# Order inside a slot of a 30-step layer-norm/FFN pipeline: TensorE turns before it multiplies, ScalarE scales and copies before SiLU and tanh

## The reference

```
def step(h, _):
    h = h + 0.01 * jnp.tanh(h)
    h = h * jax.nn.sigmoid(h)
    h = _layernorm(h, ln_w, ln_b)
    h = jnp.einsum('bsc,dc->bsd', h, W) + b
    return (h, None)
x, _ = jax.lax.scan(step, x, None, length=N_ITERS)   # N_ITERS = 30
```

## Time and profile before

| | |
|---|---|
| median of three executions | 1294.8 us |
| the profiled execution | 1294.57 us, its span 1292.8 us |
| PE busy | 1257.6 us (97% of the span) |
| DVE busy | 1189.0 us (92%) |
| ACT busy | 1005.8 us (78%) |
| POOL busy | 960.8 us (74%) |
| mean granted PE clock | 0.992 of full speed |

### The profile page before, as it was taken

How to read it: one execution, slowest core, us unless ns; L and a number is a source line. 1 busy time by engine, 2 the same in 40 slices (tenths; PEclk the granted TensorE clock), 3 DMA queues, 4 the chain that set the end, 5 groups by cost and what they waited for, 6 DMA issues and landing times.

```text
span 1292.8 us, 29543 instructions
## 1 busy us (share of the span) xinstructions
PE 1257.6 (97%) x9309; PEld 1122.5 (87%) x9309; DVE 1189.0 (92%) x2808; ACT 1005.8 (78%) x1410; POOL 960.8 (74%) x783
## 2 busy tenths in 40 slices
PE   8899999999999999689999999999999999999998
PEld 7677777777777777489999999999999999999998
DVE  7888888888888877799999999999999999999997
ACT  2455555555555555789999999999999999999995
POOL 3455555544555554489999999999999999999996
PEclk9999999999999999889999999999999999999999
DMA  6111111111111000000000000000000000000004
GB/s 192 42 42 42 49 52 54 48 41 41 41 41 41 0 1 1 1 2 0 0 0 0 0 0 0 0 0 0 0 0 0 0 0 0 0 0 0 0 0 130
DMA packets 29808, 27.71 MB, mean 21 GB/s; under 512 B 3285, under 2 KB 21464, under 8 KB 29656
## 3 DMA queue, kind: packets, MB, share of 16 engines
q1 hardware_dynamic: 29784, 27.41, 6.5%
HBM read 23.21 MB, written 4.19 MB: 21 GB/s over the span
## 4 chain that ended last, share of the span: by engine, by line
PE 83%; DVE 10%; ACT 3%; issue 3%; POOL 0%; DMA 0%; SPq 0%; DVEq 0%; ACTq 0%; POOLq 0%
PE psum L860 33%; PE psum L876 16%; PE psum L856 7%; PE psum L631 4%; PE psum L633 4%; PE psum L632 4%; PE psum L802 4%; PE psum L653 3%; PE psum L648 3%; DVE emb_n L1409 2%; DVE xh_mem L1233 1%; PE psum L642 1%; ACT emb_f L993 1%; PE psum L662 1%; DVE upd L1370 1%
## 5 line engine op out<-in xcount | busy, mean ns | idle before, releaser
L482 POOL TENSOR_TENSOR f_rs<-f_var,half_neg 128x8 f32<-128x8 f32 x240 | 395.1, 1646 | 24.5 <-DVE f_var L1299 5.4
L930 ACT ACTIVATE g_ring<-u_ring 128x1024 f32<-128x1024 f32 x240 | 407.1, 1696 | 3.1 <-DVE u_ring L1274 3.0
L953 ACT ACTIVATE y_all<-psum 128x1024 f32<-128x1024 f32 x240 | 397.2, 1655 | 8.7 <-PE psum L876 8.7
L860 PEld LDWEIGHTS psum<-w_t,y_all 128*128 128x128 f32 x2880 | 382.8, 193 | 9.4
L940 ACT ACTIVATE t_ring<-psum 128x1024 f32<-128x1024 f32 x232 | 388.1, 1673 | 3.0 <-PE psum L860 3.0
L860 PE MATMUL psum<-w_t,y_all 128*128 128x128 f32 x2880 | 388.6, 275 | 0.0
L1262 DVE BATCH_NORM_STATS2 f_stat<-g_ring 128x6 f32<-128x256 f32 x960 | 341.9, 418 | 3.5 <-ACT g_ring L930 3.5
L488 POOL TENSOR_TENSOR h_ring<-g_ring,f_rs 128x640 f32<-128x640 f32 x240 | 302.1, 1259 | 18.8
L1274 DVE SCALAR_TENSOR_TENSOR u_ring<-t_ring,psum 128x1024 f32<-128x1024 f32 x232 | 279.0, 1203 | 0.7 <-ACT t_ring L940 0.7
L876 PE MATMUL psum<-ident,h_ring 128*128 128x128 f32 (+1 forms) x1920 | 252.2, 275 | 2.4 <-issue 2.4
L947 ACT ACTIVATE h_ring<-g_ring,f_rs 128x128 f32<-128x128 f32 x240 | 248.3, 1035 | 1.6 <-POOL f_rs L482 1.6
(11 more groups left out here) (194 smaller groups left out, 2136.0 us busy)
## 6 DMA issues: line engine op xcount, KB each, us to landing
work<-in_adj_dram SPq DMA_DIRECT2D x16, 1024.0 KB, 5.4
x_tok<-in_x_dram SPq DMA_DIRECT2D x16, 256.0 KB, 5.6
out_dram<-y_all SPq DMA_DIRECT2D x7, 512.0 KB, 3.2
work<-in_L_gnn_conv_w_dram SPq DMA_DIRECT2D x1, 1088.0 KB
out_dram<-y_all SPq DMA_DIRECT2D x2, 256.0 KB, 3.5
work<-in_L_gnn_w_ih_dram SPq DMA_DIRECT2D x1, 384.0 KB
work<-in_L_gnn_w_hh_dram SPq DMA_DIRECT2D x1, 192.0 KB
work<-in_L_gnn_W_dram SPq DMA_DIRECT2D x1, 64.0 KB, 5.1
```

The source lines that it names most:

```text
L482: pool.tensor_tensor(f_rs[:, j % 4, :], f_var[:, j % 2, :], half_neg[:, 0:GT], ALU.pow).then_inc(f_pow, 1)
L860: m = pe.matmul(y_ps[k % 2][:, h, C * t:C * t + C], y_all[:, GT * k + NT * h + t, :], w1_t[:] if t < biased else w1c_t[:], start=False, st ...
L930: act.activation(g_ring[j], u_ring[j % 2], ACT.Silu).then_inc(f_silu, 1)
L953: act.activation(y_all[:, GT * j:GT * j + GT, :].rearrange("p t c -> p (t c)"), g_ps[j % 2].rearrange("p h n -> p (h n)"), ACT.Copy).then_ ...
```

## The change

In PE's slot the turns are now written ahead of the products: T(s-6), then P(s). In ACT's slot scale(s-5) and state(s-6) are written first, then silu(s-2), and tanh(s) last. DVE, POOL and the DMA queue are unchanged, and so are all waits and lags. T is line 853 now, P is lines 870 and 874.

```
@@ PE @@
             def slot(it, k):
+                before = earlier(it, k, LAG_T)
+                if before is not None:
+                    i, j, s = before
+                    pe.wait_ge(f_norm, s + 1)
+                    if ACT_TILES[j]:
+                        pe.wait_ge(f_norm_act, act_norms(i, j + 1))
+                    pe.wait_ge(f_norm_dve, dve_norms(i, j) + 1)
+                    wait(pe, f_state, s - 1)
+                    for t in range(GT):
...
+                    m.then_inc(f_turn, 1)
                 if not (isinstance(it, int) and it == 0):
...
                     m.then_inc(f_mm, 1)
-                before = earlier(it, k, LAG_T)
-                if before is not None:
...
-                    m.then_inc(f_turn, 1)
@@ ACT @@
             def slot(it, k):
-                before = earlier(it, k, LAG_S)
-                if before is not None:
-                    silu(*before[1:])
-                if not (isinstance(it, int) and it == ITERS):
-                    tanh(it, k)
                 before = earlier(it, k, LAG_A)
                 if before is not None:
                     scale(*before[1:])
                 before = earlier(it, k, LAG_T)
                 if before is not None:
                     state(*before[1:])
+                before = earlier(it, k, LAG_S)
+                if before is not None:
+                    silu(*before[1:])
+                if not (isinstance(it, int) and it == ITERS):
+                    tanh(it, k)
```

More of the change, by code:

```diff
@@ L841, in slot @@
             def slot(it, k):
+                before = earlier(it, k, LAG_T)
[7 more added lines that the diff above has]
+                    for t in range(GT):
+                        rows = P if t < GT - DVE_TILES[j] else P - 1
+                        m = pe.transpose(g_ps[j % 2][0:rows, t // NT, P * (t % NT):P * (t % NT) + P],
+                                         tiles(h_ring[j % 4])[:, t, 0:rows], ident[:])
+                    m.then_inc(f_turn, 1)
                 if not (isinstance(it, int) and it == 0):
```

## The result

The changed kernel takes 1380.52 us (median of 4, 1379.0 to 1381.57), the kernel before 1294.55 in the same comparison: ratio 1.0661, 95% interval 1.0649 to 1.0674, 86 us slower. Forecast were 1378 and a range of 1360 to 1398.

A forecast was written before the change was run, and what follows sets the result against it. DVE alone was taken to bound the kernel at 3.06 us per slot; after the change a two-slot loop through POOL and ACT needs 3.41. 1294.6 + 81.2 (232 slots) + 2.5 (edges) = 1378 us, range 1360 to 1398.

The forecast's parts named there:

- The bound before: Iterated layer of the kernel before: DVE alone bounds at 3.06 us per slot, ACT 0.01 to 0.02 behind, PE 0.07.
- The loop through POOL and ACT: Sum, variance, power, scale, state, silu, stats, sum two slots on: 6.82 us, 3.41 per slot against 3.06; +81.2 us.
- power to scale: Term of the loop: from the start of POOL's power to the start of ACT's waiting scale, 1.67 us.
- silu to stats: Term of the loop: from the start of ACT's silu to DVE's waiting stats, 1.08 to 1.25 us.
- Silu's delay: On ACT: silu's true time is its record of 1.05 us, not the mid-run record of 1.89.
- long-silu rival: ACT's silu really takes 1.89 us: loop 7.57, 3.79 per slot, +169, 1464 us; chance 0.05.
- The edges: First products behind low-clock turns, and PE entering the last iteration later: +2.5 us for both, bounds -1 and +4.
- The other loops: After the change, loops through PE (3.12 per slot) and through tanh on ACT (3.2) stay hidden behind the first.
- Through PE: ... 6.24, or 3.12 per slot: Sum, DVE's scale, turns, products, tanh, sum two slots on: hidden by ACT's loop; without that cover 14 us.
- The clock rival: PE, idle some 0.4 us per slot, drops to 1.2 GHz: 1930 us throughout, about 1650 for half the time; chance 0.04.
- Not slower: Turns fill PE's 19.2 us wait for the sum: 1278 us, or 1295 if nothing changes; chance 0.06, half each.
- The signs in the profile: Profile after: sums 3.41 apart; ACT idle before scale, DVE before stats, POOL before power, PE before turns; clock 1.00.

The follow-up runs named there:

- experiment 3: Changed kernel with silu put back ahead of scale on ACT (silu, scale, state, tanh), PE as changed: 1327.56 us, ratio 1.0257.
- experiment 5: Changed kernel with a longer power on POOL, 10 columns in place of 8, two of them spare: 1415.46 us, ratio 1.093.
- experiment 4: Changed kernel with a shorter power on POOL, 5 of 8 reciprocal roots, part of the computation left out: 1354.07 us, ratio 1.046.
- experiment 1: Kernel before with only PE's half of the change, turns ahead of products, ACT's order as before: 1672.22 us, ratio 1.2917.
- experiment 2: Kernel before with only ACT's half of the change (scale, state, silu, tanh), PE as before: 1510.58 us, ratio 1.1668.
- experiment 6: Kernel before with power on POOL edited: shorter (5 of 8 roots) 1293.54 us, ratio 0.9991; longer (10 columns) 1335.88 us, ratio 1.0313.

## Why the prediction was right

**The bound before.** It was no loop through power and not POOL: a shorter power changed next to nothing there, and another order with room changed nothing. That it was DVE, and not ACT with 0.02 less per slot, rests on DVE's missing idle time; no run shortened DVE.

**The loop through POOL and ACT** was the right one: experiment 3 breaks it by moving silu out, experiment 5 has its slope, half a microsecond per microsecond. Its length, forecast 6.82, is 6.84. Two terms were off and cancel: power to scale is 1.66 to 1.78, 1.71 in the mean, and not 1.67, and silu to stats is mostly 1.08, 1.14 in the mean, where I took 1.165. The slot is 3.42 against 3.41. The mechanism was right; that the time was met to 2.5 us is in part luck, since two slots take anything from 6.74 to 6.93.

**Silu's delay** was 1.05, as chosen; the long-silu rival (1464) is out by the slot of 3.42 and by the records of 1048 ns.

**The edges**: 2.5 forecast, 3.2 found (1.8 at the start, 1.4 at the end). At the start the first products begin 2.2 later, 555.27 for 553.07, behind turns that wait for ACT's scale and then take 1.75 at the low clock.

**The other loops.** "Through PE: ... 6.24, or 3.12 per slot" is the step that was mis-sized: it measured 6.35, by the hand-over from DVE's scale to the turns, 0.85 and not 0.70. With the cover gone it costs 33 us in experiment 3, and not 14: 3.198 less 3.069 per slot is 30 us, of which the longer gap once in eight slots is 5. And the list was incomplete: the loop of three slots at 3.27 to 3.33 was hidden 0.1 under the bound. Neither error touched the forecast, because the first loop covered both; with the shorter power of experiment 4 the same way of adding up was 25 us off.

**The clock rival** (1650 to 1930) is out for this kernel: 1.00 with PE at 92% and idle times of at most 0.7 us, and still 1.00 in experiment 1, at 69% with an idle time of some 1.5 us in each slot. But the worry had a ground. With ACT's half alone (experiment 2), PE at 79% and idle for 1.6 to 1.8 us in every other slot, the clock fell five times. What decides between these cases no run here shows.

**Not slower** is out: no piece of the loop was shorter than read by more than 0.1.

**The signs in the profile** came as listed, except that the waits of scale and stats come in every other slot, 0.5 to 0.7 each, as goes with long and short gaps in turn; that a part of scale's waits is put down to PE; and that PE waits less for DVE's scale than I said, 63.7 us in all, 0.28 per slot for 0.4.

## What to carry to other kernels

When several engines are full, a reordering inside a slot is judged by the loops of waits: add the delays from start to start around each loop, divide by the slots it spans, and compare with the fullest engine; do it for all loops within a few per cent of the bound, since the next one takes over (3.42, 3.31, 3.20 and 3.06 lay on top of one another here). Moving an instruction ahead of others takes a slot out of every loop that runs from it to one of those that it has passed; it is free only where the fullest engine's time for the slots that are left (2 x 3.06 or 3 x 3.06 here) still holds the loop. To test such a loop, lengthen one piece and look for the slope 1/n: shortening it meets the next loop (experiment 4), and lengthening it too may meet an engine that becomes full (experiment 6).

## What the runs showed of the hardware that was not expected

- An ACT record can be nearly twice as long as the work: 1676 ns on average for tanh in the kernel before, 1020 in the kernel after, with the same instruction. The starts were 0.90 to 0.95 apart in both.
- PE's granted clock stays at its upper level, 2.4 GHz, at 69% busy with an idle stretch of about 1.5 us in every slot of 4.7 (experiment 1). With 1.6 to 1.8 us idle in every other slot of 3.97 (mean) and 79% busy it stays there most of the time, but fell five times for some us between 565 and 840 us (experiment 2), each time with a gap of 6.14 to 6.46 in place of 4.9.
- From the start of DVE's last scaled tiles to the start of PE's turns that wait for them pass 0.83 to 0.86 us (0.59 of it the record).
- The loop over iterations costs 0.1 to 0.3 us per round of 8 slots once a loop of waits is the bound (3.46 for 3.28 in experiment 3, 4.92 for 4.63 in experiment 1). Under a full DVE it doesn't show: by place in the round the mean gaps lie between 3.057 and 3.068 in the kernel before.
